# The up projection of a feed-forward layer as three float32r products, with gamma and beta folded into its weights and bias

## The reference

```
w1 = (fc1_q - 128) * fc1_scales            # 256 x 1024
h  = (n * ln_gamma + ln_beta) @ w1 + fc1_bias
out = ... silu(h) @ w2 + fc2_bias ...
```

## Time and profile before

| | us |
|---|---|
| three runs | 1123.62 to 1125.34, median 1124.2 |
| the profiled execution: its own time | 1123.7 |
| its span, first to last instruction | 1121.9 |
| PE busy (90% of the span) | 1008.8 |
| DVE busy (85%) | 949.2 |
| ACT busy (77%) | 862.2 |
| POOL busy (59%) | 666.2 |

### The profile page before, as it was taken

The page is one execution under the profiler, slowest core; times in us unless marked ns, Lnnn a source line. Parts: engine busy times, 40 slices in busy tenths (PEclk is TensorE's granted clock), DMA queues, the critical chain, the costliest instruction groups (busy, mean ns, idle before and its releaser), DMA issues. The chain is left out here.

```text
span 1121.9 us, 17411 instructions
## 1 busy us (share of the span) xinstructions
PE 1008.8 (90%) x5326; PEld 715.3 (64%) x5326; DVE 949.2 (85%) x1237; ACT 862.2 (77%) x1688; POOL 666.2 (59%) x599
## 2 busy tenths in 40 slices
PE   6999999999969999987658799999999999988987
PEld 4777777777745455454436467676676757667576
DVE  7999999999954887665999999999999899999741
ACT  7768878887645666667868798898988989896843
POOL 2466666766750123124777968878696986968320
PEclk9999999999989999999779899999999999999999
DMA  6444434442505011114896666767577675776301
GB/s 187 131 126 130 127 101 138 116 135 85 142 5 185 1 38 39 56 39 116 235 166 168 129 153 130 146 151 167 137 146 164 142 163 139 145 145 131 80 2 38
DMA packets 93232, 133.84 MB, mean 119 GB/s; under 512 B 8786, under 2 KB 47698, under 8 KB 93140
## 3 DMA queue, kind: packets, MB, share of 16 engines
q1 hardware_dynamic: 93140, 132.73, 48.2%
HBM read 116.45 MB, written 14.16 MB: 116 GB/s over the span
## 5 line engine op out<-in xcount | busy, mean ns | idle before, releaser
L2260 DVE TENSOR_TENSOR_SCAN oa<-bank_a,h,oa 128x512 f32<-128x512 f32 x128 | 159.6, 1269 | 12.5 <-ACT h L1937 10.5
L2260 DVE TENSOR_TENSOR_SCAN ob<-bank_a,h,ob 128x512 f32<-128x512 f32 x128 | 160.3, 1268 | 9.3 <-ACT bank_a L1928 7.0
L1755 PE MATMUL bank_m<-w,f_h 128*128 128x256 f32 x448 | 104.7, 384 | 0.0
L40 PE MATMUL bank_m<-oa,w 128*128 128x512 f32 x224 | 103.1, 595 | 1.1 <-ACT oa L1995 0.9
L1468 POOL TENSOR_TENSOR oa<-ob,x1T 128x1024 f32<-128x1024 f32 x8 | 18.9, 2357 | 135.1 <-DVE ob L1370 135.1
L1928 ACT ACTIVATE bank_a<-dtc,A 128x512 f32<-128x512 f32 x128 | 86.7, 683 | 15.3 <-DVE ob L2260 7.6
L1928 ACT ACTIVATE bank_a<-s,A 128x512 f32<-128x512 f32 x128 | 86.5, 682 | 15.2 <-DVE oa L2260 9.1
L1755 PEld LDWEIGHTS bank_m<-w,f_h 128*128 128x128 f32 x448 | 84.8, 193 | 13.1 <-issue 2.4
L1710 PE MATMUL bank_y<-ident,ob 128*128 128x128 f32 x512 | 71.3, 285 | 19.4 <-DVE ob L2266 19.4
L1933 ACT ACTIVATE bank_c<-Cb 128x512 f32<-128x512 f32 x128 | 75.5, 590 | 16.8 <-DVE ob L2266 12.5
L2469 POOL TENSOR_TENSOR oa<-uc,Bb 128x1024 f32<-128x1024 f32 x32 | 75.7, 2367 | 20.1 <-DVE ob L2266 11.0
(11 more groups left out here) (386 smaller groups left out, 2785.4 us busy)
## 6 DMA issues: line engine op xcount, KB each, us to landing
Bb<-CB_rows SPq DMA_DIRECT2D x128, 256.0 KB, 5.2
Cb<-CB_rows SPq DMA_DIRECT2D x128, 256.0 KB, 4.9
abc<-decays SPq DMA_DIRECT2D x32, 512.0 KB, 4.6
Ebc<-ramps SPq DMA_DIRECT2D x64, 128.0 KB, 3.2
uT<-in_uT SPq DMA_DIRECT2D x8, 512.0 KB, 4.7
u<-in_u SPq DMA_DIRECT2D x8, 512.0 KB, 3.9
x_tokens<-x2s SPq DMA_DIRECT2D x8, 512.0 KB, 2.9
x_rows<-x1T SPq DMA_DIRECT2D x8, 512.0 KB, 3.4
```

Source lines behind the costliest of these rows:

```text
L40: i = e.matmul(out, w, x, start=(n == 0), stop=(n == len(pairs) - 1))
L1755: i = e.matmul(to, f_h[:, k, c * CH:(c + 1) * CH], w2[:, k, :], start=False, stop=(c % 2 == 1 and k == KF - 1))
L2260: e.tensor_tensor_scan(s[:, k, :], p_a[k][:, :], s[:, k, :], h0[:, n, k:k + 1], ALU.mult, ALU.add).then_inc(v_s, 1)
```

## The change

The weights w1 with gamma are kept as two float32r tiles, the rounded value `w1_h` and the remainder `w1_l`; the input likewise as `nT_h` and `nT_l`. The up projection is w1_h*nT_h + w1_l*nT_h + w1_h*nT_l. ACT only copies the input out of the bank (rounding it), and DVE makes the remainder (`low`, `end_low`) from the same bank. Beta times w1 is added to the bias by sixteen products with one column on PE in turn 8 of the coupling stage. The tiles into which w1's integers are loaded are now `dtc[0]` and `uc[0]`, and the coupling stage has one tile `tw` in place of two.

```diff
             loaded = [(x[:, :, :], y) for x, y in loaded]
-            loaded += [(w1[:, :, :].bitcast(I32), rows(d["f_q1"])), (w2[:, :, :].bitcast(I32), rows(d["f_q2"]))]
+            q1 = [flat(dtc[0]).bitcast(I32), flat(uc[0]).bitcast(I32)]
+            loaded += [(q1[k], rows(d["f_q1"])[:, k, :]) for k in range(KD)] + [(w2[:, :, :].bitcast(I32), rows(d["f_q2"]))]
...
                 def to_channels(b):
                     after(e, c_xT, 2 * b if b < NB - 1 else 0)
+                    if b == 0:
+                        e.wait_ge(c_w, 7)
...
                         fourth(*at(w - 1))
+                    if w == 8:
+                        e.wait_ge(c_w, 3)
+                        for m in range(KF):
+                            i = passes(e, b_x[0][:, m:m + 1], [(s1[:, k, m * P:(m + 1) * P], lb[:, k:k + 1]) for k in range(KD)])
+                        i.then_inc(c_fold, 1)
...
                         evac_channels(ended(w - 5))
+                    if w in (13, 14):
+                        k = w - 13
+                        e.wait_ge(c_w, 3)
+                        e.activation(w1_h[:, k, :], s1[:, k, :], ACT.Copy, scale=lg[:, k:k + 1]).then_inc(c_wx, 1)
...
                     e.tensor_scalar(cS[n % 2][:, :], cS[n % 2][:, :], slope[:, 0:1], shift[:, 0:1], ALU.mult, ALU.add).then_inc(c_cs, 1)
-                    after(e, c_o0, n - 1)
-                    after(e, c_o1, n - 1)
+                    after(e, c_o0, n)
+                    after(e, c_o1, n)
...
                     if w == 6:
                         e.wait_ge(ld, DMAS * len(loaded))
-                        e.tensor_scalar(w1[:, :, :], w1[:, :, :].bitcast(I32), -128.0, None, ALU.add).then_inc(c_w, 1)
+                        for k in range(KD):
+                            e.scalar_tensor_tensor(s1[:, k, :], q1[k], -128.0, s1[:, k, :], ALU.add, ALU.mult).then_inc(c_w, 1)
...
                     if w == 8:
-                        e.wait_ge(c_w, 2)
-                        e.tensor_tensor(w1[:, :, :], w1[:, :, :], s1, ALU.mult).then_inc(c_w, 1)
-                    if w == 9:
-                        e.wait_ge(c_w, 3)
+                        e.wait_ge(c_w, 4)
                         e.scalar_tensor_tensor(w2[:, :, :], w2[:, :, :], 0.5, s2, ALU.mult, ALU.mult).then_inc(c_w, 1)
                     if w == 10:
...
+                        e.wait_ge(c_fold, 1)
+                        e.tensor_tensor(b1s[:, :], b_x[0][:, 0:KF], b1, ALU.add).then_inc(c_w, 1)
...
+                    if w in (15, 16):
+                        k = w - 15
+                        e.wait_ge(c_wx, k + 1)
+                        e.scalar_tensor_tensor(w1_l[:, k, :], s1[:, k, :], lg[:, k:k + 1], w1_h[:, k, :].bitcast(F32), ALU.mult, ALU.subtract).then_inc(c_w, 1)
...
                 def up_proj(b, m):
+                    if m < 2:
+                        e.wait_ge(v_nl, 2 * b + m + 1)
+                    else:
+                        e.wait_ge(a_up, 8 * b + m - 1)
                     if m == 0:
                         e.wait_ge(a_ft, 2 * b + 2)
-                    elif m > 1:
-                        e.wait_ge(a_up, 8 * b + m - 1)
-                    passes(e, pair[m % 2][:, :], [(w1[:, k, m * P:(m + 1) * P], nT[:, k, :]) for k in range(KD)]).then_inc(pe_up, 1)
+                    ws = slice(m * P, (m + 1) * P)
+                    for k in range(KD):
+                        e.matmul(pair[m % 2][:, :], w1_h[:, k, ws], nT_h[:, k, :], start=(k == 0), stop=False)
+                        e.matmul(pair[m % 2][:, :], w1_l[:, k, ws], nT_h[:, k, :], start=False, stop=False)
+                    if m == 0:
+                        e.wait_ge(v_nl, 2 * b + 2)
+                    for k in range(KD):
+                        i = e.matmul(pair[m % 2][:, :], w1_h[:, k, ws], nT_l[:, k, :], start=False, stop=(k == KD - 1))
+                    i.then_inc(pe_up, 1)
...
                 def evac_normed(b, k):
                     after(e, pe_up, 8 * b)
                     e.wait_ge(pe_ft, 2 * b + k + 1)
-                    e.activation(nT[:, k, :], pair[k][:, :], ACT.Identity, bias=lb[:, k:k + 1], scale=lg[:, k:k + 1]).then_inc(a_ft, 1)
+                    e.activation(nT_h[:, k, :], pair[k][:, :], ACT.Copy).then_inc(a_ft, 1)
...
-                    for k in range(KD):
-                        e.activation(nT[:, k, p * DM:(p + 1) * DM], wide[p][:, k * DM:(k + 1) * DM], ACT.Identity, bias=lb[:, k:k + 1], scale=lg[:, k:k + 1]).then_inc(a_ft, 1)
+                    e.activation(nT_h[:, :, p * DM:(p + 1) * DM], wide[p][:, :].rearrange("p (k t) -> p k t", k=KD), ACT.Copy).then_inc(a_ft, 1)
...
+                def low(b, k):
+                    e.wait_ge(a_ft, 2 * b + k + 1)
+                    after(e, pe_up, 8 * b)
+                    e.tensor_tensor(nT_l[:, k, :], pair[k][:, :], nT_h[:, k, :].bitcast(F32), ALU.subtract).then_inc(v_nl, 1)
+
+                def end_low(p):
+                    e.wait_ge(a_ft, 2 * Z + p + 1)
+                    ts = slice(p * DM, (p + 1) * DM)
+                    e.tensor_tensor(nT_l[:, :, ts], wide[p][:, :].rearrange("p (k t) -> p k t", k=KD), nT_h[:, :, ts].bitcast(F32), ALU.subtract).then_inc(v_nl, 1)
...
                         scan(post, 10, 1)
                         scan(post, 11, 0)
+                    if 0 <= last < NB - 1:
+                        low(last, 0)
+                    if live(post):
                         product(post, 10)
+                    if 0 <= last < NB - 1:
+                        low(last, 1)
+                    if live(post):
                         scan(post, 11, 1)
...
                 second(Y, 1)
+                end_low(0)
                 stats6(Y, 1)
+                end_low(1)
                 end_second(0)
```

More of the change, by code:

```diff
@@ L980, in build @@
         gam, bet = vec_at["c_gamma"], vec_at["c_beta"]
-        w1, w2 = sb("w1", [P, KD, FF]), sb("w2", [P, KF, DM])
+        w1_h, w1_l = (sb(n, [P, KD, FF], F32R) for n in ("w1_h", "w1_l"))
+        w2, b1s = sb("w2", [P, KF, DM]), sb("b1s", [P, KF])
         diagD = sb("diagD", [P, KD, P])
@@ L1039, in coupling @@
             c_wh, c_wl, c_xh, c_xl = (sem(n) for n in ("wh", "wl", "xh", "xl"))
-            ld = sem("ld")
+            ld, c_fold, c_wx = sem("ld"), sem("fold"), sem("wx")
             turns = [(0, 0), (1, 0), (2, 0), (0, 1), (1, 1), (3, 0), (0, 2), (2, 1), (4, 0), (1, 2), (3, 1), (5, 0), (2, 2),
@@ L1181, in z_first @@
                 def z_first(p):
-                    e.wait_ge(c_w, 11)
+                    e.wait_ge(c_w, 12)
                     e.wait_ge(c_xT, 11 + p)
@@ L1381, in upper @@
                         e.wait_ge(c_sx, b + 1)
-                    e.tensor_tensor(dst(b, y)[:, 0, :], base, tw[n % 2][:, 0, :], ALU.add).then_inc(c_o0, 1)
+                    e.tensor_tensor(dst(b, y)[:, 0, :], base, tw[0][:, 0, :], ALU.add).then_inc(c_o0, 1)
                 def low(b, y):
@@ L1442, in weights @@
                     if w == 13:
-                        e.wait_ge(c_w, 7)
+                        e.wait_ge(c_w, 8)
                         e.tensor_tensor(bias[32:64, :], bias_f[32:64, :], bias[32:64, :].bitcast(F32), ALU.subtract).then_inc(c_w, 1)
@@ L1521, in build @@
             xl, xn, x3, x3b = (t(n, [P, NC, DM])[:, :, :] for n in ("xl", "xn", "x3", "x3b"))
-            f_h = t("f_h", [P, KF, TB])
-            state, prod, gT, nT = [oa[0], ob[0], oa[1], ob[1]], [ob[2], oa[2]], ob[3], oa[3]
+            f_h, nT_h, nT_l = t("f_h", [P, KF, TB]), t("nT_h", [P, KD, TB], F32R), t("nT_l", [P, KD, TB], F32R)
+            state, prod, gT = [oa[0], ob[0], oa[1], ob[1]], [ob[2], oa[2]], ob[3]
             st3, st4, st6 = (t(n, [P, 2, 2, 3]) for n in ("st3", "st4", "st6"))
@@ L1541, in build @@
             turned, wide, up_at = p_a, (p_c, p_m[1]), (p_y[0], p_y[1], p_a[0], p_a[1])
-            v_e, v_b, v_m = (d_sem("v_" + n) for n in ("e", "b", "m"))
+            v_e, v_b, v_m, v_nl = (d_sem("v_" + n) for n in ("e", "b", "m", "nl"))
             half = slice(0, 2), slice(2, 4)
@@ L1785, in end_up @@
                     if m == 0:
-                        e.wait_ge(a_ft, 2 * Z + 2 * p + 2)
+                        e.wait_ge(a_ft, 2 * Z + p + 1)
                     if p == 0 and m == 4:
@@ L1790, in end_up @@
                         e.wait_ge(a_up, 8 * Z + (m | 1) + 1)
-                    ts = slice(p * DM, (p + 1) * DM)
-                    passes(e, up_at[m // 2][:, (m % 2) * DM:(m % 2 + 1) * DM], [(w1[:, k, m * P:(m + 1) * P], nT[:, k, ts]) for k in range(KD)]).then_inc(pe_up, 1)
+                    ts, ws, to = slice(p * DM, (p + 1) * DM), slice(m * P, (m + 1) * P), up_at[m // 2][:, (m % 2) * DM:(m % 2 + 1) * DM]
+                    for k in range(KD):
+                        e.matmul(to, w1_h[:, k, ws], nT_h[:, k, ts], start=(k == 0), stop=False)
+                        e.matmul(to, w1_l[:, k, ws], nT_h[:, k, ts], start=False, stop=False)
+                    if m == 0:
+                        e.wait_ge(v_nl, 2 * Z + p + 1)
```

(7 more changed lines are left out.)

8 lines of the change are left out of this document (4 added, 4 removed).

## The result

The changed kernel took 1138.1 us in the median of four runs (1134.7 to 1141.1), against 1124.8 for the kernel before on the same chip (1123.6 to 1128.9): ratio 1.0112, 95% interval 1.0079 to 1.0145, so slower by 1.1%, as forecast in direction. The forecast was 1133.6, range 1127 to 1140.5. The profiled execution took 1135.7 us with a span of 1133.9, 12.0 more than before's 1121.9. Measured again beside other kernels it gave 1137.4 in six runs, in two groups: 1134.8 to 1136.0 at a mean granted clock of 0.969 to 0.970, and 1138.8 to 1139.7 at 0.965. Experiments 8, 9 and 11 bear on the two groups; what decides between them was not found.

What follows compares the result with a forecast made beforehand. The prediction took DVE's scans to pace section B of the last stage and PE the coupling stage; 7.2 - 1.0 + 5.4 - 2.2 = +9.4 us gave 1133.6 us against the median, range 1127 to 1140.5.

Steps and rivals of the forecast that it cites:

- Full blocks, +7.2: Last stage, six full blocks: two DVE remainders a block, 0.60 us each, lengthen the period; +7.2 us.
- The PE time saved: Up projection in section B: cheaper products save PE 2.7 us a block, costed at nothing because DVE's chain covers it.
- rival 1: Last stage: PE sets the period, so the change gains 2.7 us a block, giving 1108.4 us; chance 0.09.
- rival 2: Last stage: DVE's idle 3.25 us per block absorb the remainders, giving 1127.4 us; chance 0.12.
- PE's new wait for the remainder: Up projection, before the last two products of m = 0: delays about 1.2 us at most, made up by group 5.
- The neighbour that spoke of a lock: DVE's same subtraction beside GpSimd took up to 2.396 us; with one PSUM input it was claimed never blocked.
- The last loop block, -1.0: Seventh block: PE is late, saving 2.7 us while DVE ends 1.2 us later; taken as -1.0 us.
- the gate: Last loop block, where DVE waits for the last `add_up`: claimed between 2.7 us earlier and 1.2 later.
- The coupling stage, +5.4: Coupling stage: bias fold on PE +3.4 us, ACT's two weight copies +2.0, DVE's steps 0; sum +5.4.
- all is exposed: Coupling stage, turn 8: the fold stands before `first(9)`, which has no idle time, so its full +3.4 us counts.
- Rival 4: One-column products or PE's added idle time lower the clock, once per block and once at the fold: +7, 1140.6 us; chance 0.06.
- The end, -2.2: Last block behind the loop: 256-column float32r products at 0.12 us start PE's down projection earlier; -2.2 us (-3.3 to +7).

Runs made afterwards that it cites:

- experiment 8: The changed kernel measured once more, unchanged, beside the other kernels on one chip: 1137.4 us, ratio 1.0096.
- experiment 9: The changed kernel with ACT's last four normalisations of block 5 moved behind the last SiLU: 1135.2 us, ratio 1.0088.
- experiment 11: The kernel before with float32r products only in the last loop block and the last block, ACT's order as before: 1125.6 us, ratio 1.0006.
- experiment 3: The changed kernel with two float32 products in place of the three in the loop, remainders still made: 1136.4 us, ratio 1.0107.
- experiment 2: The changed kernel without the input remainder in the loop, the third product reading the rounded input: 1130.3 us, ratio 1.0052.
- experiment 6: The changed kernel with DVE's loop subtraction done twice, the first time into a tile nobody reads: 1147.4 us, ratio 1.0177.
- experiment 5: The changed kernel with the bias fold in four parts over turns 7 to 10, ACT's weight copies in turns 12 and 15: 1133.8 us, ratio 1.0061.
- experiment 10: The kernel before with float32r products in the last loop block and last block, ACT's last four block 5 normalisations behind the last SiLU: 1123.3 us, ratio 0.9978.
- experiment 7: The kernel before with float32r products only in the last block behind the loop, folded weights made on POOL: 1123.2 us, ratio 0.9976.
- experiment 4: The changed kernel with ACT's two roundings of w1 in turns 12 and 15 instead of 13 and 14: 1136.35 us, ratio 1.0104.
- experiment 1: The changed kernel without the one-column bias fold, the bias being copied instead: 1134.35 us, ratio 1.0084.
- experiment 12: The kernel before with only ACT's last four normalisations of block 5 moved behind the last SiLU: 1125.1 us, ratio 1.0000.

## Why the prediction was right, and where it missed

**Full blocks, +7.2.** Right, in mechanism and size. One remainder costs 0.58 to 0.60 us to its successor (0.60 taken); without both the period is 66.97, with both doubled 69.37. The first of the six showed 0.5 in the profiled execution and the other five 1.2 to 1.35, so 6.7; in the first one DVE waits for ACT just before both remainders (0.49 and 0.45 us), so it is not the pace there. The PE time saved was sized too large: PE's busy time in a period fell by 1.8 us (63.78 to 61.97), not 2.7. A column group behind other work takes 1.5 us to the start of the next (855.53 to 857.03 in the changed kernel), not 1.38, since its first product is followed after 0.32 us. It was costed at nothing and was worth nothing (experiment 3), which rules out rival 1; rival 2 fell with experiments 2 and 6. PE's new wait for the remainder made no term of its own.

The neighbour that spoke of a lock did not matter: the 14 remainders of the loop took 654 to 692 ns, each with a POOL instruction beside it for its whole length:

```profile
L2339 DVE TENSOR_TENSOR nT_l<-bank_m,nT_h x14: 654/675/692, 645.2 to 1054.7; 128x512 fp32r<-128x512 f32 x14
```

In the kernel before, the same subtraction with both inputs in SBUF took 1215 to 2396 ns whenever it started beside one of POOL's instructions of 128x1024 in the coupling stage. That none from x1T was slow says nothing of the source: none of those 14 had such an instruction beside it. By the Trainium skill (SBUF — State Buffer, "SBUF: two separate sides") a DVE operation with two SBUF inputs shares an exclusive lock with GpSimd; the trace agrees, in that the remainders with one input in PSUM stayed under 0.7 us.

**The last loop block, -1.0.** Measured -0.6, and that it came so close is luck: 1.35 us of it are the shorter stretch of low clock at the block's start. With the 6.8 us that the kernel before has, the block came out 1.2 us longer in experiment 5, whose last stage is the changed kernel's, and 1.0 in experiment 11. So this term has the wrong sign. The step that failed took the gate for the end of the chain. Up to the gate the forecast held in kind: with the longer low clock it comes 0.5 to 0.7 us earlier (experiments 5, 10, 11), 2.2 in the changed kernel's profile with the shorter one. What was late next was ACT: it waits 1.56 us for POOL's four small steps and normalises for 2.08 before it takes the gated product. With that moved away the silu comes 1.8 us earlier (experiment 9 against the changed kernel) and 1.7 (10 against 11). The prediction names no such wait.

**The coupling stage, +5.4.** Measured +6.8. The term that failed is the fold: 3.4 taken, 5.05 measured. Its 32 records took 3.6 us as said; the step "all is exposed" left out the clock behind them. Rival 4 had it, with a chance of 0.06 and a price of 1 us; it costs 1.5 here, and its once per block did not come (clock 1.00 over the period). The copies were 1.8 (2.0 taken), DVE's steps 0 as taken.

**The end, -2.2.** Measured -2.2 in the profiled execution and in experiment 7. Products of 256 columns follow each other after 0.12 us (1102.20, 1102.32). The estimate of 0.109 us by the Trainium skill (TensorE: Matmul & The Clock Gate, "Wait — 56ns, not 53.3ns?") was a little too small: the measured 0.12 decides, and the 0.9 us of further gain did not come. The gain is easily lost: it is 2.2 us in the profiles of experiments 3, 4 and 7 too, but in experiments 1, 2, 5, 6, 8, 9 and 11, whose clock fell somewhere behind the loop, it is 1.1 us at most (1.6 in 10).

**The sum.** 9.4 was forecast against 12.0 in the profiled execution: 1.6 too little for the fold and 0.4 for the last loop block, 0.5 too much for the full blocks and 0.2 for the copies, and 1.3 of scatter ahead of the changed code. The median is 4.5 us above the forecast, 2.4 of it above the profiled execution. The range held because it had been widened for rivals 2 and 4. What the forecast did not have is that ACT's order makes PE pause for 1.9 us where the loop ends, in place of 0.24, and that the clock often falls there:

```profile
1063.32 0.50 PE L1659 MATMUL bank_c<-bias,ones_r 128*128 128x512 f32 x1 [0.24 <-ACT ob L2017]
```

That is the kernel before's row, just behind the earlier trace rows. The same pause in all profiles:

| PE's pause there | profiles | of which the clock falls in it or up to 1.5 us behind it |
|---|---|---|
| 1.91 to 1.95 us (changed, experiments 1, 2, 4, 5, 6, 8, 11) | 8 | 6 |
| 0.15 to 0.35 us (before, experiments 3, 7, 9, 10, 12) | 6 | 0 |

Without the pause none of the five runs of experiment 9 is in the upper group, where five of ten of the changed kernel's are; 10 and 11, with twelve runs each, differ in the order alone and are 2.3 us apart. That ties the pause to the lower clock and to the time, but not all of the end's loss to the pause: some 24 us later the clock fell a second time in experiments 5, 8 and 11, and it fell there in 9 too, with no pause. What decides whether the clock falls behind the same pause (it did not in the first profile of the changed kernel, and did in the second) was not found.

## What to carry to other kernels

Where two engines are equally busy, find out which one the period runs through before moving work between them: here PE's 1.8 us a block were worth nothing and DVE's 1.2 cost all of it. Use the cheaper products only where PE is really late, in the last block, and make their weights on the engine that idles. A step that finishes early on one engine needs the next engine's order looked at, since what stands there by chance becomes the wait.

## What the runs showed that was not expected

One-column products keep PE busy by the records (2.00 of 2 us in both windows from 396 to 400) and yet, behind 32 of them in a row, the granted clock was 0.62 and 0.53; behind parts of eight it was 1.00. The changed kernel's runs lie in two groups some 3 us apart: 1134.8 to 1136.0 us in three runs at a clock of 0.969 to 0.970, 1138.8 to 1139.7 in three at 0.965. And stretches of low clock come and go from execution to execution at the same places of the same code: 6.8 or 3.4 us at the start of the last loop block, worth 1.1 to 1.35, and 3.4 or none in turn 14, worth 0.8 (experiment 8) and 1.4 (experiment 1). So the gain of a single block, read from two profiles, means little until the clock rows of that block have been compared.
